# Mixture of experts: dispatch scatters in groups of four beside the shared experts, and all shared chunks ahead of the routed blocks

## What is computed

```python
h = _L0_tok_ref(x, L0_tok_kernel)
h = h + _L0_attn_ref(_layernorm(h), ...)
h = h + _L0_ffn_ref(_layernorm(h), ...)
h = h + _L1_attn_ref(_layernorm(h), ...)
h = h + _L1_ffn_ref(_layernorm(h), ...)

def _L1_ffn_ref(x, gate_w, gate_b, sw1, sb1, sw2, sb2, rw1, rb1, rw2, rb2):
    ...
    hs = jax.nn.gelu(jnp.einsum('td,nfd->ntf', t, sw1) + sb1[:, None, :], approximate=False)
    shared = jnp.einsum('ntf,ndf->td', hs, sw2) + sb2.sum(axis=0)
    probs = jax.nn.softmax(t @ gate_w.T + gate_b, axis=-1)
    top_v, top_i = jax.lax.top_k(probs, K)
    cw = jnp.zeros_like(probs).at[jnp.arange(T)[:, None], top_i].add(top_v)
    hr = jax.nn.gelu(jnp.einsum('td,efd->etf', t, rw1) + rb1[:, None, :], approximate=False)
    oe = jnp.einsum('etf,edf->etd', hr, rw2) + rb2[:, None, :]
    routed = jnp.einsum('etd,te->td', oe, cw)
    return (shared + routed).reshape(b, s, d)
```

## Time and profile before

| | us |
|---|---|
| runs (three) | 2682.22, 2683.2, 2688.64 |
| median | 2683.2 |
| profiled execution, span from first to last instruction | 2924.9 |
| start of the experts' stage (first turn of rows) | 2003.94 |
| first routed turn of rows | 2488.45 |
| last routed scatter to `e_sums` starts | 2857.59 |

### The profile page before, as it was taken

How to read it: one execution, slowest core, us unless ns; L and a number is a source line. 1 busy time by engine, 2 the same in 40 slices (tenths; PEclk the granted TensorE clock), 3 DMA queues, 4 the chain that set the end, 5 groups by cost and what they waited for, 6 DMA issues and landing times. The chain is left out here.

```text
span 2924.9 us, 52858 instructions
## 1 busy us (share of the span) xinstructions
PE 2456.4 (84%) x16811; PEld 1878.3 (64%) x16811; DVE 2074.9 (71%) x3678; ACT 1665.1 (57%) x3131; POOL 1110.7 (38%) x1340
## 2 busy tenths in 40 slices
PE   7988799999999997559999799973112899999994
PEld 7988454444444445459999799962101788888883
DVE  3555689999999975968888778874000566787875
ACT  3345277777777786335666455451000677777773
POOL 0034022323222233356666333334776000465664
PEclk9999699999999998569999999996555999999997
DMA  3119333333333323611111230002111000577758
GB/s 82 37 46 373 72 57 57 56 56 56 56 58 58 58 33 98 191 28 37 37 38 39 73 137 0 0 1 87 50 50 59 1 1 1 168 246 236 245 177 252
DMA packets 161299, 249.22 MB, mean 85 GB/s; under 512 B 41644, under 2 KB 106901, under 8 KB 154232
## 3 DMA queue, kind: packets, MB, share of 16 engines
q1 hardware_dynamic: 128888, 208.77, 26.3%
q0 software_dynamic: 19712, 38.13, 4.4%
q10 hardware_dynamic: 12544, 0.39, 0.2%
HBM read 155.24 MB, written 93.41 MB: 85 GB/s over the span
## 5 line engine op out<-in xcount | busy, mean ns | idle before, releaser
L1014 ACT ACTIVATE probs<-score 128x748 f32<-128x748 f32 (+1 forms) x768 | 568.4, 794 | 117.5 <-PE score L839 116.2
L943 DVE TENSOR_REDUCE part_max<-to_dve 128x1 f32<-128x512 f32 (+1 forms) x768 | 480.2, 684 | 83.6 <-PE to_dve L820 83.2
L2754 DVE TENSOR_TENSOR m_hid_lo<-m_up,m_hid_hi 128x512 fp32r<-128x512 f32 x408 | 280.4, 688 | 303.2 <-issue 172.3
L820 PE MATMUL to_dve<-k_stack,q_stack 48*128 48x512 f32 (+3 forms) x1536 | 351.5, 367 | 20.1 <-DMA k_stack<-k_parts 19.3
L2650 POOL DMA_INDIRECT e_sums<-m_gated,m_row_in x216 | 212.7, 985 | 389.6 <-DVE m_gated L2772 268.7
L839 PE MATMUL score<-q_stack,k_stack 49*128 49x374 f32 (+1 forms) x1536 | 317.3, 389 | 3.1 <-ACT probs L1014 1.0
L876 PE MATMUL o_sum<-probs,v_sb 128*17 128x374 f32 (+1 forms) x3072 | 315.6, 483 | 0.1
L839 PEld LDWEIGHTS score<-q_stack,k_stack 49*128 49x128 f32 (+1 forms) x1536 | 161.9, 181 | 225.0 <-ACT probs L1014 199.7
L2732 ACT ACTIVATE m_up<-m_up,e_b 128x512 f32<-128x512 f32 x192 | 127.2, 663 | 308.0 <-remote 191.2
L820 PEld LDWEIGHTS to_dve<-k_stack,q_stack 48*128 48x128 f32 (+1 forms) x1536 | 222.9, 187 | 79.3 <-DVE part_max L943 36.6
L2693 PE MATMUL m_down<-m_hid_hi,e_w_hi 128*128 128x512 f32 x192 | 83.3, 434 | 218.5 <-issue 134.9
(11 more groups left out here) (435 smaller groups left out, 6215.3 us busy)
## 6 DMA issues: line engine op xcount, KB each, us to landing
m_weights<-e_records SPq DMA_DIRECT2D x54, 1028.0 KB
q_stack<-q_parts SPq DMA_DIRECT2D x192, 93.5 KB, 3.1
k_stack<-k_parts SPq DMA_DIRECT2D x192, 93.5 KB, 4.1
e_slots<-blank SPq DMA_DIRECT2D x54, 260.0 KB, 3.7
m_row_in<-e_slots SPq DMA_DIRECT2D x54, 260.0 KB
m_weights<-e_sums SPq DMA_DIRECT2D x16, 640.0 KB
e_records<-l_parts SPq DMA_DIRECT2D x16, 512.0 KB, 4.0
v_rows<-v_out SPq DMA_DIRECT2D x16, 408.0 KB, 5.9
```

What stands on the lines that cost most here:

```text
L820: last = pe.matmul(ring[i % RING][0:ROWS[c], at_col:at_col + keys.stop - keys.start], q_stack[its_slot][rows, j, c * P:c * P + ROWS[c]], k ...
L943: dve.tensor_reduce(part_max[0:ROWS[c], k, j, c, 0:1], ring[i % RING][0:ROWS[c], :], AX.X, ALU.max).then_inc(used, 1)
L1014: act.activation(probs[0:n, s % 2, m, 2 * j:2 * j + 2, :], score[tile][0:n, :, 0:HALF], ACT.Exp).then_inc(tile_used, 1)
L2754: dve.tensor_tensor(hid_lo[:, f % RING, :], up[f % UPS][:, :], hid_hi[:, f % RING, :].bitcast(F32), ALU.subtract).then_inc(lo_done, 1)
```

## The change

All 24 shared chunks now stand in front of the routed blocks (`EARLY = CHUNKS`), so none is left behind them, and VectorE's pair adds all stand behind the loop. The tiles are split into four parts of 24: first choice, rename, second choice of one part, then the next part. Before each group of four scatters GpSimd waits until `hid_used`, TensorE's count of finished steps, has reached five times the group's number, as long as that is at most `HELD_STEPS` = 192 - 12 = 180.

```diff
-    EARLY = 21
+    EARLY = CHUNKS
...
-    LATE = starts[shared_at[EARLY]] + 10
+    LATE = ENDS + 10
...
-        PARTS = [range(0, 7 * N // 8), range(7 * N // 8, N)]
-        scattered = [[sem(f"scattered{k}{x}") for x in range(2)] for k in range(TOP)]
+        PARTS = [range(k * N // 4, (k + 1) * N // 4) for k in range(4)]
+        GROUP, GROUP_STEPS, HELD_STEPS = 4, 5, starts[EARLY] - 12
+        scattered = [[sem(f"scattered{k}{x}") for x in range(4)] for k in range(TOP)]
...
+                def hold(at):
+
+                    steps_done = at // GROUP * GROUP_STEPS
+                    if at % GROUP == 0 and 0 < steps_done <= HELD_STEPS:
+                        pool.wait_ge(hid_used, steps_done)
+
                 def scatter(k, part):
                     for n in part:
                         top = ROWS[n % TILES]
+                        hold(part[0] * TOP + k * len(part) + n - part[0])
                         pool.indirect_dma_start(out=slots, out_offset=bass.IndirectOffsetOnAxis(
                             ap=places[0:top, k, n:n + 1], axis=0), in_=rows[0:top, n, :], in_offset=None
-                            ).then_inc(scattered[k][part is PARTS[1]], 16)
-
-                for part in PARTS:
-                    scatter(0, part)
+                            ).then_inc(scattered[k][PARTS.index(part)], 16)
+
                 for x, part in enumerate(PARTS):
+                    scatter(0, part)
                     of = slice(part[0], part[-1] + 1)
                     pool.wait_ge(scattered[0][x], 16 * len(part))
...
-                for b in range((ENDS - LATE + 1) // 2, B):
+                for b in range(B):
                     add_pair(b)
```

More of the change, by code:

```diff
@@ L2633, in scatter @@
                         top = ROWS[n % TILES]
+                        hold(part[0] * TOP + k * len(part) + n - part[0])
                         pool.indirect_dma_start(out=slots, out_offset=bass.IndirectOffsetOnAxis(
                             ap=places[0:top, k, n:n + 1], axis=0), in_=rows[0:top, n, :], in_offset=None
-                            ).then_inc(scattered[k][part is PARTS[1]], 16)
-                for part in PARTS:
+                            ).then_inc(scattered[k][PARTS.index(part)], 16)
+                for x, part in enumerate(PARTS):
                     scatter(0, part)
-                for x, part in enumerate(PARTS):
                     of = slice(part[0], part[-1] + 1)
```

## The result

The changed kernel takes 2771.5 us in the median of four runs (2768.7 to 2779.1), the kernel before 2682.7 us (2680.3 to 2688.6). The ratio is 1.0329 with a 95% interval of 1.0317 to 1.0342, so 85 to 92 us slower. The forecast was 2775 us, slower.

The account below looks back on a forecast made before the run. Scatters and shared chunks were taken to end nearly together before the first routed turn. That turn moves from 2256.4 to 2349.8 us (+93.4), less 1.5 in the tail: +91.9 on 2683.2 gives 2775 us, range 2755 to 2796.

Parts of the forecast that it names:

- The late signals: TensorE's signals during the dispatch scatters, late by 237.0 us in the profile; claimed to be scarcely in timed runs.
- The sum without them: Profiled span of the kernel before less 237.0 us of lateness: 2687.9 us, 4.7 us from the median.
- The first rival: At the experts' stage, lateness is real in timed runs and the holds remove it: 2543 us, chance 0.09.
- So what TensorE signals comes late, and nothing else: At the start of the experts' stage, only TensorE's signals were claimed late, at least 12 us at one place.
- Balance before: Before the first routed turn, scatters and chunks end nearly together; TensorE waits 0 to 10 us; 2256.4 us taken.
- The burst: After step 180, 48 scatters go out before the first routed turn; TensorE waits 60 us, rows landed at 2347.4 us.
- The holds cost the steps nothing: In the shared chunks, groups take 5.1 us against 7.4 us per five steps, so holds delay only scatters; cost 0.
- Slow restart, +2.4 us: At the first routed turn, TensorE restarts at its lower clock level: twelve matmuls 0.20 us slower each, 2.4 us.
- The tail, -1.5 us: At the end, the same chain of sixteen adds stays; 1.5 us credited at its head, 0 for VectorE's freed adds.
- The quick scatters: Rival: dispatch scatters run far quicker in timed runs; at half the beat +66.7 us, 2750 us; chance 0.04.
- the burst's own late signals: Rival: the free 48 scatters bring lateness into the timed run, 15 us more, 2790 us; chance 0.05.

Follow-up runs that it names:

- second trace before: Kernel before, unchanged, run and profiled again: median 2687.2 us, ratio 1.0006, span 2685.0 us.
- third trace: Kernel before, unchanged, run once more for its trace: 2684.2 us.
- first trace before: Original profile of the unchanged kernel before, used for the prediction: span 2924.9 us, beside a run median of 2683.2 us.

## Why the prediction was right, point by point

**The late signals are not in the runs.** Right, and it was the step on which the sign hung. The sum without them, 2687.9 us (up to 2697.9 with the wait of 0 to 10 us that it allowed), was a statement about a trace nobody had seen; the second and third traces of the kernel before have spans of 2685.0 and 2682.4 us. Its chief figure, 237.0 us, is 232.9 by comparison of traces: the wait of 4.1 us is the difference. The small rest of 7.8 us lay ahead of the stage, a place that the sum took as it was in the first trace. The trace after begins the stage at 1992.5 us, 11.4 us earlier than the first trace before, and that is most of why the span forecast for the change, 2785 us, was too long.

The first rival (late signals in the runs, 2543 us) falls with these traces. Where this case has both for one execution, the span is 1.7 to 1.8 us under the time (2766.9 and 2768.66 after, 2685.0 and 2686.7 for the second trace before).

The Trainium skill's page Runtime: NRT & Kernel Launch ("The ~15µs preamble/postamble breakdown") has the profile's total about 6.2 us above the execution time. No run here has that total, only spans from first to last instruction, so its figure is not tested; the first trace's 241.7 us beyond the runs are not such a fixed gap.

**"So what TensorE signals comes late, and nothing else" was too narrow.** The lateness grew only after the stage had begun, and it was not TensorE's alone. Four rows of the first trace before, ScalarE's waits for TensorE and GpSimd's last name change:

```profile
2020.23 0.66 ACT L2732 ACTIVATE m_up<-m_up,e_b 128x512 f32<-128x512 f32 x1 [3.07 <-PE m_up L2683]
...
2068.68 0.66 ACT L2732 ACTIVATE m_up<-m_up,e_b 128x512 f32<-128x512 f32 x1 [15.62 <-remote]
...
2235.79 0.20 POOL L2644 COPY e_rows<-e_second 128x12 f32<-128x12 f32 x1
2241.13 1.01 POOL L2634 DMA_INDIRECT e_slots<-e_rows,e_places  x1 [5.14 <-DMA v_sb<-v_rows]
```

In the program the scatter at 2241.13 us waits for GpSimd's own copies (the bracket goes by an earlier use of the same semaphore); it follows them 5.14 us later. The same place in the second trace before:

```profile
2227.91 0.20 POOL L2644 COPY e_rows<-e_second 128x12 f32<-128x12 f32 x1
2228.39 1.01 POOL L2634 DMA_INDIRECT e_slots<-e_rows,e_places  x1 [0.28 <-POOL e_rows L2644]
```

**Balance before.** I took the rows as ready at 2256.4 us, 252.5 us after the first turn; measured 251.7. The pause of 5.14 us did belong to the disturbed execution, as these rows show.

**The burst.** Predicted release of the 48 scatters 275.2 us after the first turn; measured 2267.58 - 1992.51 = 275.1. Predicted turn 343.5, measured 342.3: the first fetch has landed 2.75 us after its issue, not 3.7. TensorE's wait was to be 60 us and is 59.3. The kernels that hold to step 140, 155 or 180, or one group per four steps, follow the same sum within 2 us.

**The holds cost the steps nothing.** Right: the first routed turn less TensorE's wait there is 342.3 - 59.3 = 283.0 us, as with no holds at all. The hold's slack of 2.3 us a group covers the name changes in front.

**Slow restart, +2.4 us.** Mis-sized, not in amount but in difference: the kernel before waits 4.1 us at the same turn and restarts at the lower level too, as its rows above show. The term should have been 0 for the difference. The sum allowed a wait of 4.9 us before and put no restart behind it.

**The tail, -1.5 us.** Too small; measured -5.1 (-4.4 against the third trace). From the first routed turn to the end it takes 437.2 us in the second trace before and 432.1 after, both with a slow restart (438.5 with only the scatters changed, which keeps the three chunks behind). The 5.1 us by parts, before and after:

| | before (second trace) | after |
|---|---|---|
| first routed turn to the last scatter's start | 370.1 | 369.0 |
| from there to the first add | 8.5 | 7.3 |
| first to last of the sixteen adds | 50.0 | 47.1 |
| from there to the end | 8.6 | 8.7 |

The credit of 1.5 us was for the first row, and is 1.1. The other two rows were put at nothing. "Behind, they had cost nothing" was thus not quite so: the sixteen adds take 49.4 to 51.2 us in the three undisturbed traces with three chunks behind, and 46.5 to 47.3 in the five with all chunks in front. I had put VectorE's freed pair adds at nothing because each add waits for its pair's transfer; but from the fifth pair on a transfer waits in turn for VectorE's add of four pairs earlier, which frees its buffer, and before, that add stood among shared steps. The second add of each engine in the second trace before, then in the trace after:

```profile
2628.96 1.94 POOL L2658 TENSOR_TENSOR h<-h,m_weights 128x768 f32<-128x768 f32 x1 [0.73 <-DMA m_weights<-e_sums]
...
2632.25 1.94 DVE L2779 TENSOR_TENSOR h<-h,m_weights 128x768 f32<-128x768 f32 x1
```

```profile
2713.43 2.06 POOL L2665 TENSOR_TENSOR h<-h,m_weights 128x768 f32<-128x768 f32 x1 [0.59 <-DMA m_weights<-e_sums]
...
2715.53 0.96 DVE L2786 TENSOR_TENSOR h<-h,m_weights 128x768 f32<-128x768 f32 x1 [1.69 <-POOL h L2665]
```

Before, VectorE's add starts 1.35 us behind the end of GpSimd's and takes 1.94 us; after, 0.04 and 0.96. So the link is there; how much of the 5.1 us it accounts for was not tested apart.

The two slips, +2.4 and 3.6 us too little credit, are why 91.9 us was forecast where the traces give 342.3 - 251.7 - 5.1 = 85.5 us. The medians give 88.8. That the forecast of 2775 us came within 3.5 us of the median is in part luck: it missed the traces by 6.4 us, and the medians happen to lie 3.3 us further apart than the traces (the profiled execution after is 2.8 us under its own median).

**The quick scatters and the burst's own late signals**, the second and third rivals: the beat in undisturbed traces is the same 1.28 us, and the turn after the burst comes when the rows land. Neither took place.

## What to carry to other kernels

A pace that is set by counts must fit: 48 groups at one per five steps need 240 steps, and what the last hold leaves over goes out behind it, at the worst place, in front of the reader that waits for all of it. Where an engine's own issue rate is about the bound (192 scatters at 1.28 us, 246 us, beside 247 us until TensorE reaches the turn), a hold on it costs nearly its full length: with only the scatters changed, 81.4 us of holds moved the turn by 79.1 us. With three chunks more in front, 94.6 us of holds cost TensorE 59.3. And before a stall in a profile is mended, its span is to be held against the times of the runs: here 240 us of the profiled span were in none of them.

## What the runs showed of the hardware

- In one profiled execution ScalarE and VectorE saw TensorE's signals late, in one place by some 12 us (2146.4 to 2158.3 us). The lateness grew from about 2020 us on, 16 us after GpSimd's first scatter, and ended 18 us after the last. It was not TensorE's signals alone: GpSimd's own came 5.14 us after its copies instead of 0.28, and SyncE's first five fetches of rows took 6.16 us to issue instead of 2.23 in the second trace. The first name change, at 2128 us, was on time (0.28 us). Four other traces with 192 scatters beside the same steps and no holds (the kernel before twice, only the chunks moved, no holds) show none of it. What brings it on is open; no run here provoked it.
- After a wait of 4.1 us at a turn TensorE was at its lower clock level (granted clock 0.50, starts 0.43 us apart), as after the 59.3 us wait; with no wait there (no holds) the granted clock stayed at 1.00. A longer wait costs no more on restart than a short one: with all chunks in front it is 432.1 us from the turn to the end after 59.3 us, 431.7 and 432.5 after 42.8 and 11.4 us. Without a wait it is 429.3 and 430.9 us.
